# A decoder layer on one core: the self-attention's feature chain, score matmuls and opening rearranged

## What is computed

```python
q = (hidden_states @ Wq.T).reshape(b, t, HEADS, FEAT).transpose(0, 2, 1, 3)   # b=4, t=512, 16 heads of 16
...
def _feature_map(x, gamma, beta):
    mu = x.mean(axis=-1, keepdims=True)                   # over the 16 features of a head
    var = ((x - mu) ** 2).mean(axis=-1, keepdims=True)
    xn = (x - mu) / jnp.sqrt(var + LN_EPS) * gamma + beta
    diag = xn * xn
    off = xn[..., IU] * xn[..., JU]
    return jnp.concatenate([diag * FEAT ** (-0.5), off * (2.0 / FEAT) ** 0.5], axis=-1)
...
num = jnp.einsum('bhtf,bhtfd->bhtd', phi_q, kv_cum)       # causal: kv_cum is a running sum
den = jnp.einsum('bhtf,bhtf->bht', phi_q, jnp.cumsum(phi_k, axis=2))[..., None] + EPS
```

## Time and profile before, and how to read it

| | us |
|---|---|
| median of three runs | 1490.67 |
| lowest and highest | 1488.88, 1492.04 |
| the profiled execution | 1501.86 |
| its span (first to last instruction) | 1500.1 |
| TensorE busy in the span | 1243.3 (83%) |
| VectorE, ScalarE, POOL busy | 754.2, 582.5, 684.5 |
| mean clock granted to TensorE | 0.899 of 2.4 GHz |

### The profile page before, as it was taken

How to read it: one execution, slowest core, us unless ns; L and a number is a source line. 1 busy time by engine, 2 the same in 40 slices (tenths; PEclk the granted TensorE clock), 3 DMA queues, 4 the chain that set the end, 5 groups by cost and what they waited for, 6 DMA issues and landing times.

```text
span 1500.1 us, 20297 instructions
## 1 busy us (share of the span) xinstructions
PE 1243.3 (83%) x6416; PEld 712.3 (47%) x6416; DVE 754.2 (50%) x1328; ACT 582.5 (39%) x999; POOL 684.5 (46%) x597
## 2 busy tenths in 40 slices
PE   3488778856999899998999989999994449999970
PEld 3355454534554445544455444554543426666640
DVE  6475858536335753458624665446423432222217
ACT  3364555632444544445434444444441012222210
POOL 0132323420467674676655766666794431111111
PEclk8688897966999999999999999999996569999995
DMA  5580000010000100000000000000002921111113
GB/s 172 197 270 16 1 0 0 1 45 11 1 0 1 36 10 1 1 1 23 22 2 1 1 11 23 1 0 1 1 1 83 316 68 42 44 46 42 45 43 143
DMA packets 33007, 64.66 MB, mean 43 GB/s; under 512 B 4221, under 2 KB 22398, under 8 KB 32640
## 3 DMA queue, kind: packets, MB, share of 16 engines
q1 hardware_dynamic: 23200, 32.41, 6.6%
q10 hardware_dynamic: 6304, 22.59, 4.7%
q0 software_dynamic: 3408, 8.43, 1.6%
HBM read 52.89 MB, written 28.34 MB: 54 GB/s over the span
## 4 chain that ended last, share of the span: by engine, by line
PE 60%; DVE 20%; issue 10%; ACT 3%; POOL 2%; DMA 2%; another core or an unknown queue 1%; ACTq 1%; SPq 0%; DVEq 0%; POOLq 0%
PE PS L1582 11%; PE PS L1689 9%; PE PS L1510 9%; PE PS L1593 8%; DVE mxp L1168 5%; PE PS L1706 5%; PE PS L225 3%; PE PS L1417 2%; PE PS L1523 2%; PE PS L226 2%; PE PS L227 2%; DVE R L1148 2%; PE PS L1406 2%; PE PS L1427 2%; POOL acc L608 1%
## 5 line engine op out<-in xcount | busy, mean ns | idle before, releaser
L608 POOL TENSOR_TENSOR acc<-acc,PX 128x1024 f32<-128x1024 f32 (+1 forms) x176 | 421.2, 2393 | 161.1 <-ACT PX L846 155.2
L846 ACT ACTIVATE PX<-PS 128x1024 f32<-128x1024 f32 (+1 forms) x208 | 212.9, 1025 | 247.2 <-PE PS L1582 236.4
L1168 DVE TENSOR_REDUCE mxp<-PS 128x2 f32<-128x804 f32 x256 | 240.4, 986 | 132.3 <-PE PS L1523 131.9
L1593 PE MATMUL PS<-PX,V 128*64 128x512 f32 (+1 forms) x832 | 226.3, 623 | 0.0
L550 POOL TENSOR_SCALAR_AFFINE_SELECT A<-A 128x128 f32<-128x128 f32 x256 | 88.8, 359 | 219.8 <-ACT A L751 216.2
L1689 PE MATMUL PS<-W,XBT 128*128 x312 | 149.6, 603 | 1.3 <-ACT XBT L902 1.3
L751 ACT ACTIVATE A<-PS 128x512 f32<-128x512 f32 (+3 forms) x256 | 99.3, 437 | 98.0 <-PE PS L1417 90.9
L669 POOL DMA_INDIRECT Y<-yb,goal_u x39 | 38.4, 986 | 201.8 <-DVE yb L1327 196.7
L1417 PE MATMUL PS<-qT,kT 128*128 128x512 f32 (+3 forms) x256 | 88.0, 420 | 27.0 <-ACT A L751 21.9
L1582 PEld LDWEIGHTS PS<-QH,KH 64*128 64x128 f32 (+1 forms) x416 | 38.4, 181 | 151.3 <-issue 89.9
L1582 PE MATMUL PS<-QH,KH 64*128 64x512 f32 (+1 forms) x416 | 104.6, 499 | 3.5 <-issue 2.2
(11 more groups left out here) (261 smaller groups left out, 2138.9 us busy)
## 6 DMA issues: line engine op xcount, KB each, us to landing
W<-in_w SPq DMA_DIRECT2D x24, 512.0 KB
XB<-XG ACTq DMA_DIRECT2D x39, 129.0 KB, 2.1
yl<-Y SPq DMA_DIRECT2D x4, 1024.0 KB, 9.0
X<-in_x SPq DMA_DIRECT2D x1, 2048.0 KB, 12.1
out<-X SPq DMA_DIRECT2D x4, 512.0 KB, 2.9
xt_raw<-in_xt SPq DMA_DIRECT2D x3, 512.0 KB, 4.4
c_raw<-in_ctxt SPq DMA_DIRECT2D x6, 200.0 KB, 2.4
c_raw<-in_ctxt SPq DMA_DIRECT2D x12, 100.0 KB, 2.6
```

The costliest lines, as they stand in the source:

```text
L608: ins = pool.tensor_tensor(sums[0:r], sums[0:r], PX[0:r, (NL * p + t) % NP, :, :], ALU.add)
L846: act.activation(PX[0:r, u % NP, :, :], PS[0:r, score_buffer(u):score_buffer(u) + 2, :], ACT.Exp, scale=XD ** -0.5)\
L1168: dve.tensor_reduce(mxp[:, p % 2, :, v % NT, v // NT:v // NT + 1].rearrange("p a o -> p (a o)"), PS[:, k:k + 2, 0:BW], AX, ALU.max)\
L1593: mm = pe.matmul(PS[rows, 4, :], V[0:LROWS[j], j, P * p + XD * half:P * p + XD * half + XD], PX[0:LROWS[j], u % NP, half, :], start=(j == ...
```

## The change

Five edits, all in the self-attention.

1. **Means out of the weights.** VectorE takes the mean of each group of 16 columns out of the query and key weights once, at the start (2 reductions, 1 scaling, 2 additions, chained by the new semaphore `wch`), ahead of ScalarE's cast of the weights. The step `centre` and its three instructions per tile are gone; ScalarE squares the projection straight from PSUM, and VectorE's `normalise` reads PSUM instead of `cen`. So bank 2 is free for the next tile only when `normalise` has read it: `project_qk` waits for `nrm_ok` where it waited for `cen_ok`.
2. **Heads on row halves.** `kT` holds two heads on its two row halves like `qT`; one 128-row copy (L1009 after) replaces the two of 64 rows, and the zero fills go. The scores of two heads are two matmuls of 64 rows each, on the upper and lower half, into banks 4 and 5 (`scores`). The pair waits until both scores of the pair before are squared, and ScalarE squares both in one instruction (1024 columns at c = 0).
3. **A shorter chain per tile.** variance in slot 2i + 2 instead of 2i + 3, normalise in 2i + 3, affine in 2i + 4.
4. **Projections last.** TensorE does a slot's projections behind its values and its other steps.
5. **The opening** goes by two tiles at a time; odd tiles project into bank 6.

```diff
@@ -431,8 +431,8 @@
             ahead = {0: [("x",)], 9: [("split", 0)], 10: [("split", 1)], 11: [("split", 2)], 12: [("split", 3), ("vs", 0)],
                      13: [("vs", 1), ("turn q", 0, 0), ("turn k", 0, 0)], 14: [("vs", 2), ("turn q", 0, 1), ("turn k", 0, 1)],
                      15: [("turn q", 1, 0), ("turn k", 1, 0)]}
-            for i in range(NT):
-                for after, kind in ((1, "project v"), (1, "project qk"), (2, "centre"), (3, "variance"), (4, "normalise"), (5, "affine")):
+            for i in reversed(range(NT)):
+                for after, kind in ((1, "project v"), (1, "project qk"), (2, "variance"), (2, "centre"), (3, "normalise"), (4, "affine")):
                     ahead.setdefault(2 * i + after, []).insert(0, (kind, i))
             last = {5 + 2 * k: [("weights", k)] for k in range(4)}
...
@@ -445,13 +445,19 @@
             return [ds for ds in steps if ds[1][0] not in LATE] + [ds for ds in steps if ds[1][0] in LATE]
 
         FEATURES = ("project qk", "project v", "centre", "variance", "normalise", "affine")
-        OPENING = [("x",)] + [(kind, 0) for kind in FEATURES[0:3]]
-        for i in range(NT):
-            OPENING += [(kind, i + 1) for kind in FEATURES[0:3] if i + 1 < NT] + [(kind, i) for kind in FEATURES[3:]] \
-                + ([("split", i - 1)] if i >= 1 else [])
-        OPENING += [("split", NT - 1)] + [("vs", g) for g in range(3)] \
+        OPENING = [("x",)]
+        for two in ((0, 1), (2, 3)):
+            OPENING += [(kind, i) for i in two for kind in FEATURES[0:3]] + [("variance", i) for i in two]
+            OPENING += [("split", i - 2) for i in two if i >= 2]
+            OPENING += [("normalise", i) for i in two] + [("affine", i) for i in two]
+        OPENING += [("split", i) for i in (2, 3)]
+        OPENING += [("vs", g) for g in range(3)] \
             + [("turn " + part, g, q) for g, q in ((0, 0), (0, 1), (1, 0)) for part in "qk"]
         CLOSING = [("back", 3), ("quad", 3), ("yt", 0), ("yt", 1), ("out", 0), ("out", 1), ("stats",), ("rsqrt",), ("norm",)]
+
+        def qk_bank(t, i):
+
+            return 6 if isinstance(t, int) and t == 0 and i % 2 == 1 else 2
 
         def started(b, n, least):
 
...
                     act.wait_ge(lo_ok, 8 * t)
                 act.copy(Vn[:, i, :], bank(3, D)).then_inc(v_out, 1)
-                act.wait_ge(cen_ok, NT * t + i + 1)
-                act.activation(feat[:, i, :], cen[:, i % 2, :], ACT.Square).then_inc(sq_ok, 1)
+                act.wait_ge(qk_mm, NT * t + i + 1)
+                act.activation(feat[:, i, :], bank(qk_bank(t, i)), ACT.Square).then_inc(sq_ok, 1)
 
             def deviation(t, i):
                 act.wait_ge(var_ok, NT * t + i + 1)
...
                     cross_weight_high(i)
 
             def squared_scores(b, n):
-                for j in range(4):
-                    u, c = 4 * n + j, n % NT
-                    act.wait_ge(sc_mm, 64 * b + u + 1)
+                for two in range(2):
+                    u, c = 4 * n + 2 * two, n % NT
+                    act.wait_ge(sc_mm, 64 * b + u + 2)
                     if started(b, u, 8):
                         act.wait_ge(av_mm, 16 * b + (u - 8) // 4 + 1)
-                    act.activation(A[:, u % 8, P * c:T], PS[:, 4 + u % 2, P * c:T], ACT.Square,
-                                   scale=0.25).then_inc(sqr_ok, 1)
+                    act.activation(A[:, u % 8:u % 8 + 2, P * c:T], PS[:, 4:6, P * c:T], ACT.Square,
+                                   scale=0.25).then_inc(sqr_ok, 2)
 
             def attention(b, first, more):
...
@@ -763,6 +767,8 @@
             for s in OPENING:
                 step(0, s)
                 if s == ("x",):
+                    act.wait_ge(wch, 3)
+                    act.copy(WSh[:, :, 0:3 * D], raw[:, 0:2, 0:3 * D]).then_inc(w_hi, 1)
                     act.wait_ge(ld_w, 16 * N_LDW)
                     act.copy(WSh[:, :, 3 * D:], raw[:, 0:2, 3 * D:]).then_inc(w_hi, 1)
...
             dve.memset(VS[:, :, :, SF:], 1.0).then_inc(const_dve, 1)
-            dve.memset(as32(kT[64:P, :, 0:4:2, :]), 0.0).then_inc(const_dve, 1)
-            dve.memset(as32(kT[0:64, :, 1:4:2, :]), 0.0).then_inc(const_dve, 1)
+            groups = [raw[:, c, 0:2 * D].rearrange("p (g f) -> p g f", f=SF) for c in range(KC)]
+            dve.wait_ge(ld_q, 16)
+            for c in range(KC):
+                ins = dve.tensor_reduce(w_mean[:, c, :], groups[c], AX, ALU.add)
+            ins.then_inc(wch, 1)
+            dve.wait_ge(wch, 1)
+            dve.tensor_scalar(w_mean[:, :, :], w_mean[:, :, :], -1.0 / SF, None, ALU.mult).then_inc(wch, 1)
+            dve.wait_ge(wch, 2)
+            for c in range(KC):
+                ins = dve.tensor_tensor(groups[c], groups[c], w_mean[:, c, :].unsqueeze(2).broadcast_to([P, 32, SF]), ALU.add)
+            ins.then_inc(wch, 1)
+            dve.wait_ge(wch, 3)
             dve.wait_ge(w_hi, 1)
...
@@ -945,18 +961,6 @@
 
                 ins.then_inc(s, 1)
                 dve.wait_ge(s, value)
-
-            def centre(t, i, wait):
-
-                at = 2 * (NT * t + i)
-                v = bank(2).rearrange("p (g f) -> p g f", f=SF)
-                dve.wait_ge(qk_mm, NT * t + i + 1)
-                chain(dve.tensor_reduce(g_mean[:, i % 2, :], v, AX, ALU.add), cch, at + 1)
-                chain(dve.tensor_scalar(g_mean[:, i % 2, :], g_mean[:, i % 2, :], -1.0 / SF, None, ALU.mult), cch, at + 2)
-                if wait:
-                    dve.wait_ge(feat_ok, NT * t + i - 1)
-                dve.tensor_tensor(cen[:, i % 2, :].rearrange("p (g f) -> p g f", f=SF), v,
-                                  g_mean[:, i % 2, :].unsqueeze(2).broadcast_to([P, 32, SF]), ALU.add).then_inc(cen_ok, 1)
 
             def variance(t, i):
...
@@ -977,7 +981,9 @@
                 dve.tensor_tensor(rs, rs, tt, ALU.mult).then_inc(fn_ok, 1)
                 dve.wait_ge(fn_ok, NT * t + i + 1)
                 v = cen[:, i % 2, :].rearrange("p (g f) -> p g f", f=SF)
-                dve.tensor_tensor(v, v, rs.unsqueeze(2).broadcast_to([P, 32, SF]), ALU.mult).then_inc(nrm_ok, 1)
+                if started(t, i, 2):
+                    dve.wait_ge(feat_ok, NT * t + i - 1)
+                dve.tensor_tensor(v, bank(qk_bank(t, i)).rearrange("p (g f) -> p g f", f=SF), rs.unsqueeze(2).broadcast_to([P, 32, SF]), ALU.mult).then_inc(nrm_ok, 1)
 
             def affine(t, i):
...
@@ -1000,8 +1006,7 @@
 
             def turn(b, g, q):
                 dve.wait_ge(tk_mm, 8 * b + 2 * g + q + 1)
-                dve.tensor_copy(kT[0:64, g % 2, 2 * q, :], bank(1, rows=64)).then_inc(kT_ok, 1)
-                dve.tensor_copy(kT[64:P, g % 2, 2 * q + 1, :], PS[64:P, 1, :]).then_inc(kT_ok, 1)
+                dve.tensor_copy(kT[:, g % 2, q, :], bank(1)).then_inc(kT_ok, 1)
 
             def quad_out(b, g):
                 dve.wait_ge(av_mm, 16 * b + 4 * g + 4)
...
         @block.tensor
         def _(pe):
             pe.wait_ge(const_pool, 3)
-            pe.wait_ge(const_dve, 3)
+            pe.wait_ge(const_dve, 1)
             pe.wait_ge(w_lo, 1)
 
             def project_qk(t, i):
 
                 pe.wait_ge(xt_lo, t + 1)
-                if started(t, i, 1):
-                    pe.wait_ge(cen_ok, NT * t + i)
+                if isinstance(t, int) and t == 0:
+                    if i >= 2:
+                        pe.wait_ge(nrm_ok, i - 1)
+                else:
+                    pe.wait_ge(nrm_ok, NT * t + i)
                 rows = slice(P * i, P * i + P)
                 for c in range(KC):
-                    mm = split3(pe, bank(2), xt_h[:, c, rows], xt_l[:, c, rows], WSh[:, c, 0:2 * D], WSl[:, c, 0:2 * D],
+                    mm = split3(pe, bank(qk_bank(t, i)), xt_h[:, c, rows], xt_l[:, c, rows], WSh[:, c, 0:2 * D], WSl[:, c, 0:2 * D],
                                 c == 0, c == KC - 1)
                 mm.then_inc(qk_mm, 1)
...
                 for i in range(NT):
                     mm = pe.transpose(PS[:, bk, P * i:P * i + P],
                                       as32(src[:, i, h:h + 2, :, :]).rearrange("p h s f -> p (h s f)"), ident[:, :])
                 mm.then_inc(done, 1)
 
-            def score(b, n, j):
-                g, c, u = n // NT, n % NT, 4 * n + j
-                if c == 0 and j == 0:
+            def scores(b, n, two):
+
+                g, c, u = n // NT, n % NT, 4 * n + 2 * two
+                if c == 0 and two == 0:
                     pe.wait_ge(qT_ok, 8 * b + 2 * g + 2)
-                    pe.wait_ge(kT_ok, 16 * b + 4 * g + 4)
+                    pe.wait_ge(kT_ok, 8 * b + 2 * g + 2)
                 if started(b, u, 2):
-                    pe.wait_ge(sqr_ok, 64 * b + u - 1)
-                pe.matmul(PS[:, 4 + u % 2, P * c:T], kT[:, g % 2, j, P * c:P * c + P],
-                          qT[:, g % 2, j // 2, P * c:T], start=True, stop=True).then_inc(sc_mm, 1)
+                    pe.wait_ge(sqr_ok, 64 * b + u)
+                for half in range(2):
```

(14 more changed lines are left out.)

26 lines of the change are left out of this document (11 added, 15 removed).

## The result

The changed kernel takes 1516.31 us (median; 1514.62 to 1517.95), the kernel before 1489.78 beside it (1486.94 to 1492.04): a ratio of 1.0179 with a 95% interval of 1.0156 to 1.0203, 26.5 us slower. I had forecast 13 us slower. The sign was right, and so was the mechanism that I gave most room to; half of the loss was missing from the sum.

What follows compares the result with a forecast made beforehand. No engine is full; waits between engines bound the kernel. Per steady batch 10.6 + 4.0 - 9.6 = +5.0, three batches +15, opening -2: +13 on 1490.7, say 1503 us; own range 1495 to 1512, with rivals 1476 to 1518.

Steps and rivals of the forecast that it cites:

- The three waits: Steady batches, slots 3, 5, 7: TensorE waits for normalise to read bank 2; 3.2, 3.2, 4.2 us, 10.6 a batch.
- The clock: Projections behind the bank 2 waits run at the lower clock three times in four, 1.8 us each: 4.0 a batch.
- What it gives back: Savings per steady batch: slot 1 3.3, centring 3.8, key copies 1.4, less VectorE work 1.1; sum 9.6 us.
- slot 1's wait: Tile 0's projection, moved behind scores and values, no longer waits 2.15 us for tokens: 3.3 us less per steady batch.
- The score pairs: Self-attention scores: 4.6 us saved, 3.1 lost to 34 row-use changes; taken at zero, between -1.5 and +3 a batch.
- rival D: Score row halves do not run at once, nothing saved: 1521 us; chance 0.15 together with C.
- The alternation: Score squares: two of 1024 columns leave a 0.5 us gap, costing only in the few slots that ScalarE paces.
- The last batch: Batch without projections: shorter key copies -1, squares' gaps +1, zero in sum; expected at 45 to 47 us.
- The opening: Before the first batch: start some 2.9 us later, then faster by tile pairs; -2 us, bounds -4 and +1.
- A: Slots 3, 5, 7: waits fall where nobody needs TensorE, half of 10.6, no lower clock; 1476 us, chance 0.28.
- B: Steady batches: waits come as computed but the clock stays up, +1.0 a batch; 1492 us, chance 0.12.
- C: Scores: row-use changes cost 0.2 us, not 0.09; pair gaps also in last batch; 1518 us, 0.15 together with rival D.

Runs made afterwards that it cites:

- The filler: Changed kernel with six unread TensorE products computed into bank 3 ahead of each re-issued projection; 1507.57 us, ratio 1.0131 to before.
- Experiment 1: Changed kernel with VectorE copying each projection out of bank 2 ahead of variance, normalise working on the copy; 1490.26 us, ratio 0.9942 to before.
- experiment 10: The kernel of experiment 5 with the query and key projection back in the middle of its slot; 1485.63 us, ratio 0.9906 to before.
- experiment 5: Changed kernel with the early copy out of bank 2 and the before kernel's full-row score scheme; 1468.54 us, ratio 0.9864 to before.
- experiment 2: Changed kernel with the before kernel's score scheme (full rows, four single squares, two key copies); 1506.95 us, ratio 1.0087 to before.
- The square of experiments: Changed kernel with the copy, four score forms, ratios to before: full rows single squares 0.9864 and 0.9854, paired 1.0005; row halves single 0.9883, paired 0.9942.

## Why the prediction was half right

In the order of its steps.

**The three waits** were forecast at 3.2, 3.2 and 4.2 us and came at 3.05, 2.61 and 3.98 in the second batch, 9.3 a batch over all three against 10.6. Right, by the steps given: which instructions stand on VectorE between the square and the read that frees the bank.

**The clock** was forecast at 4.0 a batch. The nine projections behind the waits take 35.1 us in the changed kernel, where nine at the upper level would take 9 x 2.3 = 20.7: 4.8 a batch. The filler gives back 2.7 net, or some 4 without what it costs in slot 1. The mechanism was right, and so was the size as far as the runs can tell. Waits and clock together are 9.3 + 4.8 = 14.1 a batch against 14.6. Experiment 1 fits: the copy moves the end of the last value product from 342.53 to 305.5 us, 37 us, 12 a batch, after the 2.8 us a batch that the copies cost VectorE.

**What it gives back**, 9.6 a batch, was perhaps too much. VectorE's relief was measured (11.7 us of 12), slot 1's wait went (experiment 10 prices it at 2 us a batch), and there is no wait of ScalarE for `cen` left. But with the waits gone experiment 5, which lacks only edit 2, has steady batches of 65 us against 71 (68 and 65 when it ran again): some 6 a batch, at the cost of a copy of 0.69 us a tile on VectorE. I had 8.2 for the same items (3.3 + 3.8 + 1.1). If all four copies lie on the path the true figure is near 9, if none does it is 6; the runs do not say which. I added each of TensorE's stalls in full. In experiment 5 TensorE still waits in each steady batch for the low half of the attention's output (`y_l`, 2.3 to 2.5 us) and for the residual in `X` (1.9); waits of this kind were in the trace of before, and I did not ask what would be late next.

**The score pairs** are the step that failed: "That costs only in the few slots that ScalarE paces. I take the whole edit at zero." Its bound of +3 a batch was about the true value. In the changed kernel edit 2 costs 0.9% (experiment 2 against the changed kernel), some 13 us or over three per batch, as much as the sum lacked: of that, 4.9 us lie in the last batch and about 3 in each of the others, where 8.0 was measured and 5.0 forecast. Two things were wrong in it.
- The saving on TensorE. I had 4.6 us from running halves at once, less 3.1 for 34 changes of row use at 0.09 us. At the upper clock, from the start of a 512-column pair to the next instruction is 0.44 us on row halves (171.35 to 171.79 above) and 0.57 on full rows. For 384 columns the shortest cases are 0.37 and 0.35, for 256 columns 0.31 and 0.32, for 128 columns 0.25 and 0.17. Eight pairs of each a batch save 8 x (0.13 - 0.02 + 0.01 - 0.08) = 0.3 us. Both halves do run at once (rival D is out): from 128 to 512 columns a pair grows by 0.19 us on row halves and by 0.40 on full rows. But each pair carries 0.2 us over its columns (0.44 less 512 columns at 2.4 GHz, 0.21), more than a change into row halves and one out of them at 0.09 each. The Trainium skill (TensorEngine Tiling, § Key Properties) says that a change of tiling mode drains TensorE. The trace agrees that there is a fixed cost, about 0.2 us a pair where other work stands on both sides; that all of it is this drain is not shown. I had the rule and priced it from a place where one change follows a run of row halves.
- The alternation. I took a gap of 0.5 us "in the few slots that ScalarE paces". The square of experiments shows 0.6 to 1.5% for pairing alone, and 5 to 8 us of it in the last batch. In the 512-column slot at the upper clock it was 0.5 us; 0.6% is 9 us, or 0.14 us in each of the 64 slots, so such gaps, and the lower clock that goes with them, lie bare in many more slots than I thought.

**The last batch** was forecast at zero and lost 4.9 us. It has no projections, and single squares take all of the loss out (46.2 to 46.5 us), so this is the pairing of edit 2, at a clock of 0.81 instead of 0.93. Of the list of signs, "the last batch at 45 to 47 us" was the one that failed (it took 51.3), together with "steady batches of 74 to 78" (80 and 81).

**The opening** was forecast at -2 and came at -2.6, counted to the first 384-column score product (the turns begin at 44.51, half a us below my 45 to 48; TensorE starts 3.0 us later, forecast 2.9).

**The rivals.** A and B are out: the waits were not covered and the clock fell. C, at 1518, is nearest to the 1516.3, but that is mostly luck. Its price was all for changes of row use, 3.7 a batch, and the runs show about 0.2 us for a whole pair and at most 0.3% of the kernel for row halves. What it had right is the half that it gave no price: the gaps of pairs are on the path in the last batch too. I gave it with D 0.15. I had counted the gap itself: the earlier trace rows has four single squares in 2.28 us, 2.8 from the first score product with ScalarE's 0.54 before them. Two double squares written out step by step (pair, square, pair, square: 0.5 + 1.02 + 0.5 + 1.02) are 3.0; measured were 3.3 at the upper clock (experiment 1) and 3.9 at the lower (327.53 to 331.45). What I left out was to do this for every slot, and at the lower clock.

Sum with the measured terms: waits 9.3, clock 2.7 to 4.8, edit 2 3 to 4, less 6 to 9 given back, is 6 to 12 a batch. The measured 8.0 lies in it, but the terms are not known well enough to close the sum further. With 8.0 a batch, 4.9 for the last one and -2.6 for the opening it is 26.

**The version to keep** is experiment 5: the change with the projection copied out of its bank ahead of `variance` and the score scheme of before, 0.9864 and 0.9854 of before in two comparisons, 21 and 23 us faster than before and 3.2% faster than the changed kernel (0.9854 / 1.0179).

**Left open.** Why edit 2 costs a quarter of its later price in the before kernel. And whether the bank could be freed without a copy, by a second bank for the projections in the steady batches, as in the opening: all eight banks are in use there, and it wasn't tried. Nor was `normalise` ahead of the layer norm on VectorE, which might shorten the wait of slot 7 without a copy.

## What to carry to other kernels

When a step is folded away, look at which signal used to free its input buffer: here the centring was VectorE work, and it was also what emptied the PSUM bank two steps early. Four copies a batch, 0.7 us each, were worth 12 us a batch here, because TensorE, the busiest engine, stood behind the bank. And two buffers that are filled and read in turn were worth more than one instruction over both: write out one slot of producer and consumer, instruction by instruction, before pricing such a merger at zero.

## What was unexpected of the hardware

Six products that nobody needs, put into a wait of 3 us, made the kernel 0.5% faster: the projections behind took 2.3 us instead of 4.1.

Two 64-row score products run at once, but it hardly pays for short ones among full-row work: at the upper clock, from the pair's start to the next instruction it is 0.44, 0.37, 0.31 and 0.25 us for 512, 384, 256 and 128 columns, against 0.57, 0.35, 0.32 and 0.17 on full rows.

The square of two banks in one instruction of 1024 columns takes 1.03 us and two of 512 in a row 1.14 (2.28 for four), so merging them saves ScalarE 0.1 us. It cost more than that in what must wait for both: 5 to 8 us in the last batch.
